# Two-layer attention and expert kernel on one core: split expert weights kept in DRAM, crossbar transposes in the ternary layer, expert groups of 64 rows in two lanes

## The chip, the cores and the metric

One Trainium2 chip, one core of it. The metric is the device time of one execution in microseconds (us), the median of several. Engines are called PE (matrix), PEld (its weight load), DVE (vector), ACT (scalar), POOL (GpSimd) and SP (the queue that issues most DMAs).

## The reference

Four blocks follow each other on x of 2 x 1024 tokens by 512, each as `x = layernorm(x + block(x))`:

```
x = _layernorm(x + _L0_attn_ref(...))   # causal attention, 32 query heads, 8 key heads, rope
x = _layernorm(x + _L0_ffn_ref(...))    # ternary layer, 512 -> 2048 -> 512
x = _layernorm(x + _L1_attn_ref(...))   # linear attention, 16 heads, silu gates
x = _layernorm(x + _L1_ffn_ref(...))    # 16 experts, 2 per token, plus a shared expert

def bitlinear(x, w):                    # the ternary layer's product
    xn = layer_norm(x)                  # then clipped a little under its row's largest |x|
    return einsum('bsd,od->bso', absmax_quant(xn), ternarize_weights(w))
h = gelu(bitlinear(x, w_fc)); y = bitlinear(h, w_proj)

gu = einsum('th,ehj->etj', x, w_gate_up)        # j = 2 x 352
y = einsum('eti,eih,te->th', silu(g) * u, w_down, combine) + swiglu(x @ shared_gate_up) @ shared_down
```

## The kernel before, in words

Tokens are worked on in 16 tiles of 128 rows. fp32 values enter matmuls as a high and a low fp16 part; a product of two split operands takes three matmuls (high-high, high-low, low-high). Each stage is a `Phase` with one hand-written instruction stream per engine. `run_tiles` and `unrolled` write a software pipeline: in iteration s the pair (lag, fn) works on tile s - lag, in the order in which the pairs stand in the list, so that this list is the order of the engine's queue. Semaphores tie the streams; `after` waits for a buffer to come free. The stages are: preparation, twice (projection, attention, output), `ternary_ffn` (lines 804 to 966), `linear_weights`, twice (`linear_features`, `linear_output`), `route`, `dispatch`, `sparse_experts` (1737 to 1944) and `shared_and_combine`.

In `ternary_ffn` a tile's row goes through x_stats and x_norm (with the clip at line 800) on DVE, the high part on ACT (893) and the low part on POOL (957), 8 transposes on PE and a copy out of PSUM on DVE (926), 32 matmuls (849), gelu on ACT (900), statistics and h_norm (717, 794, 800) on DVE, high part on ACT (906), low part on POOL (962), 32 transposes on PE (861), copied out of PSUM half by ACT (908) and half by DVE (885), 32 matmuls (871), residual and norm on DVE.

In the last block `route` picks two experts per token, and `dispatch` sorts the 4096 token-expert pairs into groups of GS = 128 rows that belong to one expert each, while PE computes the first half of the shared expert. There are NG = 48 groups, since an expert's last group may be part empty. `owner` holds each group's expert; `fresh` is 1 where it differs from that of the group before. `sparse_experts` takes a group per step, from STREAMS = 3 streams in turn: stream r works through groups 16r to 16r + 15 and has its own weight buffers. SP reads owner and fresh into registers and issues the loads of the fp32 weights, which are skipped where fresh is 0 (`cond`). In every step, loaded or not, ACT and DVE split the 128 x 2816 gate-up weights and the down weights into high and low parts (1857, 1863, 1864, 1905, 1921, 1923). PE order of a step: first half of the gate-up product, transposes of the hidden rows, second half, transposes of the next tokens, down product:

```
unrolled(NG, [(2, gate), (3, tr), (2, up), (1, xt), (3, down)])             # PE
unrolled(NG, [(1, gate_lo), (2, swiglu), (1, xevac), (2, down_lo)])         # DVE
unrolled(NG, [(1, gate_hi), (2, tanh), (3, hevac), (2, down_hi), (2, hhi), (3, yevac)])  # ACT
```

`shared_and_combine` computes the second half of the shared expert, whose weights are loaded and split at the end of `sparse_experts`, and gathers the expert rows.

## Time and profile before

| | |
|---|---|
| median of 3 runs | 2094.9 us (2094.39 to 2102.55) |
| the profiled execution | 2098.51 us, its span 2096.7 us, mean granted clock 0.93 |
| PE, DVE, ACT, POOL busy | 80%, 70%, 48%, 27% of the span |
| DMA | 105.96 MB, mean 51 GB/s |
| ternary_ffn, first to last instruction | 774.8 to 1103.8 |
| linear_features, twice | 1129.1 to 1223.0, 1281.7 to 1374.4 |
| dispatch | 1491.2 to 1591.0 |
| sparse_experts | 1594.3 to 1975.9 |
| shared_and_combine | 1987.2 to 2091.4 |

The span runs from the first to the last instruction of the profiled execution; the metric of that execution is 1.8 us longer. The parts after the table's stages are barriers and the smaller stages. A group of instructions is named by its line in the kernel, its engine, and the tensors written and read.

### The profile page before, as it was taken

Reading aid. Unit: us, or ns where it says so; the run is one execution under the profiler, and the core shown is the slowest. Engines: PE = TensorE matmul, PEld = TensorE weight load, DVE = VectorE, ACT = ScalarE, POOL = GpSimd, SP = SyncE. Lnnn points to the kernel's source line nnn. Section 1 sums busy time; section 2 is a strip of 40 time slices with the busy share of each in tenths; the row PEclk is TensorE's granted clock in tenths of the full one; section 3 lists DMA queues with packets and bytes.
Section 4 is the critical chain, followed back from the end, with each engine's and each line's share of the span. In section 5 each row is a group of like instructions: output and inputs, shape, how many; then the busy total and the mean of one; then the engine's idle time right before and its main releaser. Section 6 shows DMA issues by size and latency. Waiting matters only on the chain. (4 is left out here: it accounts for less than half of the span.)

```text
span 2096.7 us, 35409 instructions
## 1 busy us (share of the span) xinstructions
PE 1678.1 (80%) x13401; PEld 864.9 (41%) x13401; DVE 1463.9 (70%) x2115; ACT 997.4 (48%) x1549; POOL 571.1 (27%) x568
## 2 busy tenths in 40 slices
PE   0579999777999858888984977974696888888697
PEld 0353333344333223444441543543463555555364
DVE  3558998446898478999963364364624999999667
ACT  4345777434677713333333222222133777777532
POOL 0250000252000033344321122123261444444255
PEclk9889999998999989999996988996798999999899
DMA  8000000000000000000002000002004665345234
GB/s 298 1 2 2 2 2 2 1 1 1 2 2 2 2 1 1 1 0 0 1 1 91 1 1 1 1 1 96 32 2 144 195 195 153 113 154 183 94 102 139
DMA packets 49393, 105.96 MB, mean 51 GB/s; under 512 B 7096, under 2 KB 10392, under 8 KB 48720
## 3 DMA queue, kind: packets, MB, share of 16 engines
q1 hardware_dynamic: 37632, 75.99, 10.4%
q0 software_dynamic: 7424, 21.00, 3.9%
q10 hardware_dynamic: 4176, 6.82, 0.9%
q8 instruction: 103, 1.69, 0.3%
q14 instruction: 58, 0.48, 0.1%
HBM read 149.68 MB, written 21.01 MB: 81 GB/s over the span
## 5 line engine op out<-in xcount | busy, mean ns | idle before, releaser
L624 ACT ACTIVATE attn_prob<-attn_ps_t 128x512 f32<-128x512 f32 x576 | 312.6, 595 | 127.9 <-PE attn_ps_t L591 126.3
L643 DVE TENSOR_REDUCE attn_mx<-attn_ps_s 128x2 f32<-128x1024 f32 (+3 forms) x304 | 342.8, 1163 | 41.5 <-PE attn_ps_s L572 38.0
L136 PE MATMUL sparse_ps_g<-sparse_wg,sparse_xT 128*128 128x352 f16 x1152 | 190.5, 316 | 54.7 <-DVE sparse_xT L1900 54.7
L604 PE MATMUL attn_ps_o<-attn_prob,V 128*32 128x256 f32 x2304 | 174.8, 389 | 3.6 <-ACT attn_prob L624 2.7
L1905 DVE SCALAR_TENSOR_TENSOR sparse_wg<-sparse_raw_g,sparse_wg 128x2816 f16<-128x2816 f32 x48 | 148.4, 3092 | 37.9 <-ACT sparse_wg L1857 37.8
L136 PEld LDWEIGHTS sparse_ps_g<-sparse_wg,sparse_xT 128*128 128x128 f16 x1152 | 107.8, 99 | 128.8 <-DVE sparse_xT L1900 77.7
L778 POOL TENSOR_TENSOR wo_o<-O,wo_o 128x512 f16<-128x512 f32 (+1 forms) x16 | 18.4, 1153 | 496.0 <-ACT wo_o L750 495.9
L1942 POOL TENSOR_TENSOR sparse_h<-sparse_hid,sparse_h 128x352 f16<-128x352 f32 x48 | 87.7, 1826 | 217.4 <-ACT sparse_h L1876 217.4
L1021 PE MATMUL lin_ps_z<-w,lin_xT 128*128 128x512 f16 x576 | 136.2, 387 | 0.0
L1857 ACT ACTIVATE sparse_wg<-sparse_raw_g 128x2816 f16<-128x2816 f32 x48 | 122.0, 2541 | 17.2 <-DMA sparse_raw_g<-in_L_ffn_w_gate_up_dram 17.2
L849 PE MATMUL ffn_ps_fc<-wfcT,ffn_xT 128*128 128x512 f16 x512 | 123.6, 393 | 8.1 <-DVE ffn_xT L926 8.1
L591 PE MATMUL attn_ps_t<-QT,KT 64*128 64x256 f16 x1152 | 112.3, 273 | 18.6 <-ACT attn_prob L624 11.4
L871 PE MATMUL ffn_ps_y<-wprojT,ffn_hT 128*128 128x512 f16 x512 | 116.2, 386 | 10.6 <-issue 8.8
L572 PE MATMUL attn_ps_s<-KT,QT 64*128 64x512 f16 (+3 forms) x768 | 115.2, 336 | 2.1 <-DVE attn_mx L643 2.1
L1845 PE MATMUL sparse_ps_y<-sparse_wd,sparse_hT 128*128 128x512 f16 (+1 forms) x432 | 102.7, 383 | 1.0 <-ACT sparse_hT L1883 1.0
L908 ACT ACTIVATE ffn_hT<-ffn_ps_h 128x1024 f16<-128x1024 f16 x32 | 32.8, 1024 | 138.2 <-PE ffn_ps_h L861 138.2
L1021 PEld LDWEIGHTS lin_ps_z<-w,lin_xT 128*128 128x128 f16 x576 | 53.3, 99 | 70.3 <-issue 15.6
L591 PEld LDWEIGHTS attn_ps_t<-QT,KT 64*128 64x128 f16 x1152 | 39.0, 94 | 100.0 <-ACT attn_prob L624 45.1
L871 PEld LDWEIGHTS ffn_ps_y<-wprojT,ffn_hT 128*128 128x128 f16 x512 | 50.0, 99 | 71.4 <-issue 14.2
L604 PEld LDWEIGHTS attn_ps_o<-attn_prob,V 128*32 128x32 f32 x2304 | 49.3, 108 | 69.9 <-issue 37.5
L849 PEld LDWEIGHTS ffn_ps_fc<-wfcT,ffn_xT 128*128 128x128 f16 x512 | 49.9, 100 | 65.7 <-DVE ffn_xT L926 8.9
L962 POOL TENSOR_TENSOR ffn_h<-ffn_hn,ffn_h 128x2048 f16<-128x2048 f32 x16 | 65.0, 4065 | 37.4 <-ACT ffn_h L906 37.4
(320 smaller groups left out, 3407.2 us busy)
## 6 DMA issues: line engine op xcount, KB each, us to landing
sparse_raw_g<-in_L_ffn_w_gate_up_dram SPq DMA_DIRECT2D x48, 1408.0 KB
sparse_raw_d<-in_L_ffn_w_down_dram SPq DMA_DIRECT2D x48, 512.0 KB
y_d<-sparse_y SPq DMA_DIRECT2D x48, 256.0 KB, 3.6
sparse_raw_d<-in_L_ffn_w_down_dram SPq DMA_DIRECT2D x48, 192.0 KB
prep_w_fc<-in_L_ffn_w_fc_dram SPq DMA_DIRECT2D x4, 1024.0 KB, 15.6
X<-in_L_attn_x_dram ACTq DMA_DIRECT2D x1, 4096.0 KB, 39.6
prep_w_proj<-in_L_ffn_w_proj_dram SPq DMA_DIRECT2D x4, 1024.0 KB, 22.4
x_d<-route_x SPq DMA_DIRECT2D x16, 256.0 KB, 2.0
```

The source lines that it names most:

```text
L136: last = pe.matmul(out, a(k), b(k), start=(k == 0 and n == 0), stop=(k == chunks - 1 and n == 2))
L572: last = pe.matmul(banks[par][:, h, :], QT[s, pair + h, qt * P:(qt + 1) * P], KT[s, (pair + h) // 2, c * 512:c * 512 + n], start=not diago ...
L591: last = pe.matmul(ps_t[:, (2 * g + par) % 3, i, :], KT[s, j, kt * P:(kt + 1) * P], QT[s, 2 * j:2 * j + 2, qt * P:(qt + 1) * P], start=kt ...
L604: last = pe.matmul(ps_o[32 * jj:32 * jj + 32, 256 * half:256 * half + 256], V[:, kt, 4 * jg + jj, :], prob[(2 * q + jj // 2) % 4][:, half, ...
L624: act.activation(prob[g % 4][:, par, :, :], ps_t[:, (2 * g + par) % 3, :, :], ACT.Exp, scale=HD ** -0.5).then_inc(exp_done, 1)
L643: dve.tensor_reduce(mx[x % 2][:, c, :, at:at + per], ps_s[:, 2 * (r % 2):2 * (r % 2) + 2, 0:per * n].rearrange("p e (h k) -> p e h k", k=n ...
L849: last = pe.matmul(ps_fc[n][:, :], xT[u][:, part, k, :], m.wfcT[:, k, n * D:(n + 1) * D], start=(k == 0 and part == 0), stop=(k == KC - 1 ...
L871: last = pe.matmul(ps_y[:, :], hT[u][:, part, k, :], m.wprojT[:, k, :], start=(k == 0 and part == 0), stop=(k == NK - 1 and part == 1))
L1021: last = pe.matmul(out, xT[:, a, k, :], m.w1[:, b, i, k, :], start=False, stop=(k == KC - 1 and n == 2))
L1845: last = pe.matmul(ps_y[u][:, :], hT[u][0:size, a, k, :], wd[u][0:size, c, k, :], start=(k == 0 and n == 0), stop=(k == 2 and n == 2))
L1857: act.activation(wg[u][:, 0, :, :], raw_g[r][:, :, :], ACT.Copy, scale=WS).then_inc(gh_done, 1)
L1905: dve.scalar_tensor_tensor(wg[u][:, 1, :, :], raw_g[r][:, :, :], WS, wg[u][:, 0, :, :], ALU.mult, ALU.subtract).then_inc(gl_done, 1)
```

## The change

Three edits.

**The ternary layer** is written out without loops. Both transposes leave PE: SP issues one crossbar DMA transpose of a tile's x parts (128 x 1024 fp16) and two of its hidden parts (128 x 2048 fp16 each), from SBUF to SBUF. The copies out of PSUM go. The 128 x 2048 normalisation moves from DVE to ACT (scale and bias per row, the bias made by a small product on POOL), both low parts move from POOL to DVE, the second product has two PSUM banks, and the lags are shorter (down product at 6 instead of 7).

**The expert weights** are split once. `ExpertSplit` takes 7 pieces per expert (four of gate-up, three of down) through a ring of 6 buffers: SP loads a piece, ACT makes the high part, DVE the low part, SP stores both to DRAM tables `gate_d` and `down_d`. Experts 0 to 5 are done during the first `linear_features` (42 pieces over 8 tiles), 6 to 11 during the second, 12 to 15 and the shared second half during `dispatch` (35 pieces over 10 of its iterations). There, the work stands last in each iteration of ACT and DVE.

**The sparse stage** has groups of 64 rows, 80 of them, in STEPS = 40 steps: lane 0 takes the first 40 groups on rows 0 to 63, lane 1 the last 40 on rows 64 to 127, each with three streams. Weights come split, so ACT and DVE convert nothing. Each product is a pair of matmuls with a 64-column stationary operand, one per lane, which write the two halves of the PSUM partitions. SP reads owner and fresh for every lane and for gate-up and down apart. The low part of the hidden rows moves from POOL to DVE. The shared expert's second half is loaded after the last output.

```
-GS = P
+LANES = 2
+GS = P // LANES
 STREAMS = 3
-NG = -(-(B * N * TOPK // GS + NE - 1) // STREAMS) * STREAMS
+STEPS = -(-(B * N * TOPK // GS + NE - 1) // LANES)
+NG = LANES * STEPS
 MOST = B * N // GS
...
-    return s % STREAMS * (NG // STREAMS) + s // STREAMS
+    return sum(len(range(r, STEPS, STREAMS)) for r in range(s % STREAMS)) + s // STREAMS
...
+            @block.sync
+            def _(sp):
+                def xt(t):
+                    u = t % 2
+                    sp.wait_ge(xh_done, t + 1)
+                    sp.wait_ge(xl_done, t + 1)
+                    after(sp, fc_done, (t - 1) * NB)
+                    sp.dma_start_transpose(out=xT[u][:, :, :, :].rearrange("p a k c -> p (a k) c"),
+                                           in_=x2[u][:, :, :].rearrange("p a n -> p (a n)")).then_inc(xt_in[u], 16)
+
+                def ht(part):
+                    def fn(t):
+                        u = t % 2
+                        sp.wait_ge(hl_done if part else hh_done, t + 1)
+                        after(sp, y_done, t - 1)
+                        sp.dma_start_transpose(out=hT[u][:, part, :, :], in_=h2[u][:, part, :]).then_inc(ht_in[u][part], 16)
+                    return fn
+
+                unrolled(NT, [(3, xt), (5, ht(0)), (5, ht(1))])
+
...
+                def proj(t):
+                    u = t % 2
+                    after(pe, r_done, t - 1)
                     for part in range(2):
+                        pe.wait_ge(ht_in[u][part], 16 * (t // 2 + 1))
                         for k in range(NK):
-                            last = pe.matmul(ps_y[:, :], hT[u][:, part, k, :], m.wprojT[:, k, :],
+                            last = pe.matmul(ps_y[u][:, :], hT[u][:, part, k, :], m.wprojT[:, k, :],
                                              start=(k == 0 and part == 0), stop=(k == NK - 1 and part == 1))
...
+                unrolled(NT, [(4, fc), (6, proj)])
...
+                def h_norm(t):
+                    u = t % 2
+                    act.wait_ge(shift_done, t + 1)
+                    after(act, hl_done, t - 1)
+                    act.activation(hn[u][:, :], h[u][:, :, :].rearrange("p n k -> p (n k)"), ACT.Identity,
+                                   scale=ln_h.rstd[u][:, :], bias=shift[u][:, :]).then_inc(hn_done, 1)
+
+                unrolled(NT, [(4, gelu(0, 1, 2, 3)), (5, hhi), (2, xhi), (4, h_norm)])
...
+                    dve.tensor_tensor(x2[u][:, 1, :], xn[u][:, :], x2[u][:, 0, :], ALU.subtract).then_inc(xl_done, 1)
...
+                def h_clip(t):
+                    dve.wait_ge(hn_done, t + 1)
+                    q_h.apply(dve, hn[t % 2][:, :], t, t % 2)
+
+                def hlo(t):
+                    u = t % 2
+                    dve.wait_ge(hh_done, t + 1)
+                    after(dve, ht_in[u][1], 16 * (t // 2))
+                    dve.tensor_tensor(h2[u][:, 1, :], hn[u][:, :], h2[u][:, 0, :], ALU.subtract).then_inc(hl_done, 1)
...
-                turn = lambda g: evacuate(dve, dve.tensor_copy, ht_evac_d, g)
-                run_tiles(dve, NT, [(6, h_norm), (9, norm), (8, residual), (7, turn(1)), (5, h_stats), (7, turn(3)),
-                                    (3, x_evac), (1, x_norm), (0, x_stats)])
...
+                unrolled(NT, [(5, h_clip), (8, norm), (7, residual), (1, x_norm), (4, h_stats), (5, hlo), (2, xlo), (0, x_stats)])
...
-                run_tiles(pool, NT, [(8, lambda t, u: ln_r.root(pool, t, u)), (5, lambda t, u: ln_h.root(pool, t, u)),
-                                     (6, hlo), (2, xlo), (0, lambda t, u: ln_x.root(pool, t, u))])
+                def h_root(t):
+                    u = t % 2
+                    after(pool, hn_done, t - 1)
+                    pool.wait_ge(ln_h.s_var, t + 1)
+                    pool.tensor_tensor(ln_h.rstd[u][:, :], ln_h.var[u][:, :], m.minus_half[:, :], ALU.pow).then_inc(ln_h.s_rstd, 1)
+                    pool.wait_ge(back_done, t + 1)
+                    pool.wait_ge(ln_h.s_rstd, t + 1)
+                    pool.tensor_tensor(shift[u][:, :], back[u][:, :], ln_h.rstd[u][:, :], ALU.mult).then_inc(shift_done, 1)
+
+                unrolled(NT, [(7, lambda t: ln_r.root(pool, t, t % 2)), (4, h_root), (0, lambda t: ln_x.root(pool, t, t % 2))])
+
...
+class ExpertSplit:
...
+    RING = 6
...
+    def load(self, sp, i):
+        e, k, kd, rows, width = self.piece(i)
+        after(sp, self.lo_done, i - self.RING + 1)
...
+    def store(self, sp, i):
+        e, k, kd, _, width = self.piece(i)
+        sp.wait_ge(self.lo_done, i + 1)
...
+        sp.dma_start(table[e * P:(e + 1) * P, at * 2 * width:(at + 1) * 2 * width],
+                     self.parts[i % self.RING][:, 0:2 * width]).then_inc(self.stored[i % self.RING], 16)
+
+    def transfers(self, sp):
+
+        lag = self.RING - 2
+        for i in range(self.count + lag):
+            if i < self.count:
+                self.load(sp, i)
+            if i >= lag:
+                self.store(sp, i - lag)
...
+    def high(self, act, i):
+        u, turn = i % self.RING, i // self.RING
+        _, _, _, rows, width = self.piece(i)
+        act.wait_ge(self.raw_in[u], 16 * (turn + 1))
+        after(act, self.stored[u], 16 * turn)
+        act.activation(self.part(i, 0), self.raw[u][0:rows, 0:width], ACT.Copy, scale=WS).then_inc(self.hi_done, 1)
+
+    def low(self, dve, i):
+        _, _, _, rows, width = self.piece(i)
+        dve.wait_ge(self.hi_done, i + 1)
+        dve.scalar_tensor_tensor(self.part(i, 1), self.raw[i % self.RING][0:rows, 0:width], WS, self.part(i, 0),
+                                 ALU.mult, ALU.subtract).then_inc(self.lo_done, 1)
+
...
+    def spread(self, fn, eng, tiles, slot=0, slots=1):
+
+
+        def at(t):
+            turn = t * slots + slot
+            for i in range(turn * self.count // (tiles * slots), (turn + 1) * self.count // (tiles * slots)):
+                if t < tiles:
+                    fn(eng, i)
+        return at
 
...
+        split = ExpertSplit(f, m, d, b * LIN_EXPERTS, LIN_EXPERTS)
...
-                run_tiles(act, TB, [(0, xhi), (2, nonlinear), (3, kt_hi)])
+                unrolled(TB, [(0, of(xhi)), (2, of(nonlinear)), (3, of(kt_hi)), (0, split.spread(split.high, act, TB))])
...
-                run_tiles(dve, TB, [(1, xevac), (2, features), (3, kt_lo)])
+                unrolled(TB, [(1, of(xevac)), (2, of(features)), (3, of(kt_lo)), (0, split.spread(split.low, dve, TB))])
...
+                pe.wait_ge(m.shared_in, 32)
...
+        split = ExpertSplit(f, m, d, 2 * LIN_EXPERTS, NE + 1 - 2 * LIN_EXPERTS)
...
+                unrolled(NT, [(1, lambda t: half.swiglu(dve, t)), (4, split.spread(split.low, dve, 10, 0, 2)), (1, table_part),
+                              (3, lambda t: half.accumulate(dve, t)), (4, split.spread(split.low, dve, 10, 1, 2))])
...
+                split.transfers(sp)
...
+                def weights(s, rows, bufs, sem):
+                    r = s % STREAMS
+                    for lane in range(LANES):
+                        g = lane * STEPS + group_of(s)
                         e = sp.value_load(m.owner[0:1, g:g + 1], min_val=0, max_val=NE - 1)
                         fresh = None
                         if s >= STREAMS:
                             fresh = sp.value_load(m.fresh[0:1, g:g + 1], min_val=0, max_val=1)
+                        sp.dma_start(bufs[lane][r][:, :], rows[bass.ds(e, 1), :, :].rearrange("e p n -> p (e n)"),
+                                     cond=fresh).then_inc(sem[r], 16)
+
+                def gates(s):
+                    after(sp, gu_done, 2 * (s - STREAMS) + 2)
+                    weights(s, gate_rows, m.wgate, g_in)
+
+                def downs(s):
+                    after(sp, y_done, s - STREAMS + 1)
+                    weights(s, down_rows, m.wdown, d_in)
+
+                def outputs(s):
+                    sp.wait_ge(y_evac, s + 1)
+                    sp.dma_start(y_rows[group_of(s)], y[s % 2][:, :]).then_inc(y_out[s % 2], 16)
+
+                unrolled(STEPS, [(0, gates), (1, downs), (5, outputs)])
+                free = (STEPS - STREAMS) % STREAMS
+                sp.wait_ge(y_done, STEPS - STREAMS + 1)
+                sp.dma_start(m.wgate[0][free][:, :], gate_rows[NE]).then_inc(m.shared_in, 16)
+                sp.dma_start(m.wdown[0][free][:, :], down_rows[NE]).then_inc(m.shared_in, 16)
...
+                    for k in range(KC):
+                        for i, (a, c) in enumerate(((0, 0), (0, 1), (1, 0))):
+                            for lane, rows in enumerate(lanes):
+                                w = m.gate_part(m.wgate[lane][r], c, k, n)
+                                last = pe.matmul(ps_g[u][n][rows, :], xT[u][:, a, k, rows], w,
+                                                 start=(k == 0 and i == 0), stop=(k == KC - 1 and i == 2),
+                                                 skip_group_check=LANES > 1)
+                    last.then_inc(gu_done, 1)
...
-                    pe.wait_ge(gl_done, t + 1)
+                    pe.wait_ge(g_in[t % STREAMS], 16 * LANES * (t // STREAMS + 1))
...
-                unrolled(NG, [(2, gate), (3, tr), (2, up), (1, xt), (3, down)])
+                unrolled(STEPS, [(2, gate), (3, tr), (2, up), (1, xt), (3, down)])
...
-                unrolled(NG, [(1, gate_hi), (2, tanh), (3, hevac), (2, down_hi), (2, hhi), (3, yevac)])
-                shared_high(act, m, shared_g, raw_d[free], w_in, wh_done)
+                unrolled(STEPS, [(2, tanh), (3, hevac), (2, hhi), (3, yevac)])
...
+                unrolled(STEPS, [(2, swiglu), (2, hlo), (1, xevac)])
```

How the instructions stand on three engines, before and now. On DVE, the end of an iteration of the ternary layer, before (L885 and L926 are copies out of PSUM, ffn_hn the normalised hidden rows):

```order
L885 COPY ffn_hT<-ffn_ps_h 128x1024
L700 BN_STATS ffn_lnh_stats<-ffn_h 128x6 x4
L703 MEMSET ffn_lnh_pad 128x1
L704 BN_AGGR ffn_lnh_mv<-ffn_lnh_stats 128x2
L706 TENSOR_SCALAR ffn_lnh_var<-ffn_lnh_mv 128x1
L885 COPY ffn_hT<-ffn_ps_h 128x1024
L926 COPY ffn_xT<-ffn_ps_x 128x1024
L717 TENSOR_SCALAR ffn_xn<-X,ffn_lnx_mv,ffn_lnx_rstd 128x512
```

and now:

```order
L702 BN_STATS ffn_lnh_stats<-ffn_h 128x6 x4
L705 MEMSET ffn_lnh_pad 128x1
L706 BN_AGGR ffn_lnh_mv<-ffn_lnh_stats 128x2
L708 TENSOR_SCALAR ffn_lnh_var<-ffn_lnh_mv 128x1
L937 TENSOR_SCALAR ffn_back<-ffn_lnh_mv 128x1
L947 TENSOR_TENSOR ffn_h<-ffn_hn,ffn_h 128x2048
L930 TENSOR_TENSOR ffn_x<-ffn_xn,ffn_x 128x512
```

The copies are gone and the two low parts (L947, L930) have come from POOL; L717 of the hidden rows has left DVE.

On PE, a step of the sparse stage, before:

```order
L136 MATMUL sparse_ps_g<-sparse_wg,sparse_xT 128x352 x12
L1810 MATMUL sparse_ps_x<-ident,sparse_xg 128x128 x8
L1845 MATMUL sparse_ps_y<-sparse_wd,sparse_hT 128x512 x9
L136 MATMUL sparse_ps_g<-sparse_wg,sparse_xT 128x352 x12
L1835 MATMUL sparse_ps_h<-ident,sparse_h 128x128 x2
```

and now:

```order
L1930 MATMUL sparse_ps_g<-wgate,sparse_xT 64x352 x24
L1920 MATMUL sparse_ps_x<-ident,sparse_xg 128x128 x8
L1962 MATMUL sparse_ps_y<-wdown,sparse_hT 64x512 x18
L1930 MATMUL sparse_ps_g<-wgate,sparse_xT 64x352 x24
L1950 MATMUL sparse_ps_h<-ident,sparse_h 128x128 x2
```

The order is the same; the products have twice the matmuls on half the rows, and the transposes between them stay whole.

On SP, from one output to the next gate-up load, before:

```order
L1798 DMA y_d<-sparse_y 128x512
L1778 TENSOR_LOAD owner
L1778 ISA x2
L1781 TENSOR_LOAD fresh
L1781 ISA x2
L1783 ISA
L1783 DMA sparse_raw_g<-in_L_ffn_w_gate_up_dram 128x4x704
```

and now:

```order
L1902 DMA y_d<-sparse_y 2x64x512
L1885 TENSOR_LOAD owner
L1885 ISA x2
L1888 TENSOR_LOAD fresh
L1888 ISA x2
L1889 ISA
L1889 DMA wgate<-gate_d 128x5632
L1885 TENSOR_LOAD owner
L1885 ISA x2
L1888 TENSOR_LOAD fresh
```

The sequence from owner to DMA, once per step before, now stands four times between two outputs (two lanes, gate-up and down).

## Rows read from the trace of the kernel before

**Rows 1.** Stages: stretch, length, busy PE, PEld, DVE, ACT, POOL, clock, DMA, GB/s:

```profile
774.00:1105.00 331.00, 272.99 (x1664) 139.33 (x1664) 291.68 (x480) 112.24 (x129) 122.58 (x80) 0.95 0.00 1
1129.00:1226.00 97.00, 90.49 (x472) 45.03 (x472) 34.18 (x54) 25.72 (x45) 17.50 (x16) 0.94 0.00 1
1490.00:1594.00 104.00, 96.67 (x627) 57.65 (x627) 42.35 (x85) 28.75 (x64) 44.94 (x48) 0.98 0.02 2
1594.00:1983.00 389.00, 318.68 (x2256) 186.34 (x2256) 341.15 (x290) 292.00 (x387) 146.30 (x96) 0.97 0.52 166
```

**Rows 2.** Groups of DVE in the sparse stage (busy us, mean ns, idle before):

```profile
L1905 DVE SCALAR_TENSOR_TENSOR sparse_wg<-sparse_raw_g,sparse_wg 128x2816 f16<-128x2816 f32 x48 | 148.4, 3092 | 37.9 <-ACT sparse_wg L1857 37.8
L1921 DVE SCALAR_TENSOR_TENSOR sparse_wd<-sparse_raw_d,sparse_wd 128x1024 f16<-128x1024 f32 x48 | 58.4, 1216 | 0.0
L1900 DVE COPY sparse_xT<-sparse_ps_x 128x1024 f16<-128x1024 f16 x48 | 32.9, 686 | 0.0
```

**Rows 3.** Timeline of PE: start us, us, work, [idle before]; sparse stage, then the next:

```profile
1608.11 4.29 PE L136 MATMUL sparse_ps_g<-sparse_wg,sparse_xT 128*128 128x352 f16 x14 [6.72 <-DVE sparse_xT L1900]
...
1814.30 1.95 PE L136 MATMUL sparse_ps_g<-sparse_wg,sparse_xT 128*128 128x352 f16 x12
1816.53 2.11 PE L1845 MATMUL sparse_ps_y<-sparse_wd,sparse_hT 128*128 128x512 f16 x9
1819.67 1.96 PE L136 MATMUL sparse_ps_g<-sparse_wg,sparse_xT 128*128 128x352 f16 x12 [1.03 <-DVE sparse_xT L1900]
1821.86 1.36 PE L136 MATMUL sparse_ps_g<-sparse_wg,sparse_xT 128*128 128x352 f16 x8
...
1987.18 5.14 PE L136 MATMUL moe_ps_g<-ws_g,xT 128*128 128x352 f16 x17 [11.88 <-PEq L106]
```

**Rows 4.** Timeline of PE: fp32 matmuls on quarters and on all columns:

```profile
250.37 0.64 PE L604 MATMUL attn_ps_o<-attn_prob,V 128*32 128x256 f32 x8
250.94 0.39 PE L572 MATMUL attn_ps_s<-KT,QT 64*128 64x512 f16 x2
...
1154.86 1.05 PE L1065 MATMUL lin_ps_kv<-lin_v,lin_k 128*128 128x128 f32 x8
1155.74 0.60 PE L1072 MATMUL lin_ps_k<-consts,lin_k 128*128 128x128 f32 x4
```

**Rows 5.** Groups of PE's weight loads, by form:

```profile
L1835 PEld LDWEIGHTS sparse_ps_h<-ident,sparse_h 128*96 128x96 f16 x96 | 11.8, 123 | 0.0
L604 PEld LDWEIGHTS attn_ps_o<-attn_prob,V 128*32 128x32 f32 x2304 | 49.3, 108 | 69.9 <-issue 37.5 <-ACT attn_prob L624 25.9
```

**Rows 6.** Timeline of SP's DMA issues in the sparse stage, and its register loads:

```profile
1618.82 0.07 SPq L1789 DMA_DIRECT2D sparse_raw_d<-in_L_ffn_w_down_dram  x1
1620.34 0.07 SPq L1783 DMA_DIRECT2D sparse_raw_g<-in_L_ffn_w_gate_up_dram  x1
...
1739.51 0.34 SPq L1798 DMA_DIRECT2D y_d<-sparse_y  x1
1742.01 0.07 SPq L1783 DMA_DIRECT2D sparse_raw_g<-in_L_ffn_w_gate_up_dram  x1
...
L1781 SPq TENSOR_LOAD <-fresh x45: 261/1012/1132, 1603.6 to 1945.1; - x45
```

**Rows 7.** Ternary layer: groups, then min/median/max ns of single instructions:

```profile
L800 DVE TENSOR_SCALAR ffn_xn<-ffn_xn,ffn_qx_limit 128x512 f32<-128x512 f32 x16 | 43.3, 2706 | 0.6
...
L717 DVE TENSOR_SCALAR ffn_hn<-ffn_h,ffn_lnh_mv,ffn_lnh_rstd 128x2048 f32<-128x2048 f32 x16 | 28.6, 1787 | 0.8 <-issue 0.6
...
L800 DVE TENSOR_SCALAR ffn_xn<-ffn_xn,ffn_qx_limit x16: 545/4331/4428, 778.1 to 1006.6; 128x512 f32<-128x512 f32 x16
...
L962 POOL TENSOR_TENSOR ffn_h<-ffn_hn,ffn_h x16: 4057/4066/4073, 814.5 to 1084.2; 128x2048 f16<-128x2048 f32 x16
```

**Rows 8.** DMA: a stretch at full load, then a queue's packets, MB, share in 160:380:

```profile
20.00:40.00 20.00, 0.00 (x0) 0.00 (x0) 5.56 (x2) 18.46 (x17) 0.00 (x0) 1.00 1.03 404
...
q1 hardware_dynamic: 1062, 0.06, 0.3%
```

325 lines of the change are left out of this document (140 added, 185 removed).

## Prediction

> **What bounds the kernel now.** I read the stages first [rows 1], then inside the two stages that change most the groups of instructions and the timelines.
>
> In the sparse stage DVE is busy 341 of 389 us and PE 319. One step takes 7.56 us: the second gate-up halves start at 1814.30 and 1821.86 [rows 3]. Of it DVE spends 3.09 + 1.22 us on two of the three low parts of weights and 0.69 on a copy [rows 2]; the third low part and the gating fill the rest. PE waits 1.03 us per step for DVE's copy [rows 3], so alone it would need 6.5 us. DVE, chained to ACT's conversions, bounds the stage; 48 steps pay the conversion, although the experts are 16.
>
> In the ternary layer DVE is busy 292 of 331 us and PE 273. Part of DVE's time is not its own: the clip of 128x512 takes 0.545 us at best and 4.33 in the median, about the 4.07 of POOL's low part, beside which it runs [rows 7]. In linear features PE is busy 90 of 97 us, DVE 34 and ACT 26, in dispatch PE 97 of 104 [rows 1]: PE bounds both, and nothing moves over the DMA.
>
> **Ternary layer.** From DVE's 291.7 us go: the stalls of the clip, 16 x (2.706 - 0.545) = 34.6; the normalisation, 28.6 [rows 7]; 48 copies (32 of hidden, 16 of x) of the form that takes 0.686 [rows 2], 32.9. It gets both low parts. 128x1024 takes 1.216 and 128x2816 3.092 [rows 2], that is 1.05 ns per element, so 128x2048 costs 2.29 and 128x512 about 0.69; with 0.15 for the bias's sign, 16 x 3.13 = 50. Sum 245.6, **46 less**. PE loses 40 transposes per tile and keeps 64 matmuls of 128x512, about 64 x 0.215 = 13.8 us (9 such matmuls take 2.11 with the 0.17 of the last one's drain [rows 3]), under DVE's 15.3. ACT gets 1.9 us per tile and loses two copies. POOL keeps only one-column work. The order of the lists hides ACT's normalisation behind DVE's low parts (4.0 us), but leaves nothing over; I take 46, and 30 to 56 as its ends.
>
> The transposes have no row. Lower bound: 1.25 MB per tile at the 404 GB/s of a loaded DMA [rows 8], 3.2 us. Upper bound: the smallest packets of the trace, 64 bytes, 1062 of them in 0.3% of 16 engines over 220 us [rows 8], or 10 ns each: if a transpose goes in such packets, 20480 of them over 16 engines are 12.8 us. Both lie under 15.3 us per tile, and the lags leave about 7 us of slack behind a transpose, so it costs nothing. If it goes in 32-byte pieces, it is 25.6 us and bounds the layer (rival C). I take the hidden case, since the source is read along rows of 2 and 4 KB.
>
> The Trainium skill speaks against this change: VectorE: DVE Perf Modes, "The three transpose paths", gives 1309 ns for a 128x128 block by DMA against 390 on PE. Taken as a rate, 40 blocks are 52 us per tile and the sum would be 590 us worse. DMA: Bandwidth & Descriptors, "Latency and other measured facts", gives 261 GB/s, which would be 5 us per tile and hidden. No row here shows either; I read the first as a latency.
>
> **Splitting.** An expert has four 128x704 and three 128x512 pieces: DVE 4 x 0.88 + 3 x 0.68 = 5.6 us by the same line [rows 2]. Six experts in 97 us of linear features bring DVE from 34 to 68 us, ACT likewise from 26 to about 57, both under PE's 90. DMA: 6 x (2.11 read + 2.23 written) = 26 MB, 65 us at 404 GB/s. Covered in the middle; if that cover fails, the stage goes to the DMA's pace. At the start it isn't: five pieces (1.8 MB, 4.5 us, and 2 of latency) must land and be split before ACT makes the next tile's high part, on which PE's second transposes wait. Twice 6 us, and 2 each for late chunks: **+16** (+8 to +60). Dispatch gets 28 us of DVE over ten iterations of 6 us, and 22 MB, 54 us of DMA in them: **+5** (0 to +25).
>
> **Sparse stage.** POOL's low part goes to DVE, whose step is then about 2.2 us; ACT's is 2.5. Three candidates remain.
> PE: 24 pairs of gate-up, 9 of down, 14 transposes. If the lanes of a pair run beside each other, the step is PE's 6.5 us. Do they? Eight fp32 matmuls of 256 columns on quarters of the array start at 250.37 and are over at 250.94, 0.57 us; eight of 128 columns on the whole array take 0.88 [rows 4], so 256 columns one after another would take 1.76. Four quarters give 3.1 of 4. Bounds per step therefore 6.5 and, at that 0.77, 8.2; switching between halves and whole array four times a step, I take 7.1.
> SP: from the end of the y issue at 1739.85 to the end of the next gate-up issue at 1742.08 it takes 2.23 us, of which the fresh load is 1.01; without a DMA just ahead the same sequence takes 1.50 (1618.89 to 1620.41) [rows 6]. With nothing else on SP, it now stands four times a step: 2.23 + 3 x 1.50 + 0.38 for y = 7.1. An issued load adds 0.3, and 0.75 to the fresh load after it. 16 experts over six lane streams are at most 21 loads of each kind, 15 after the first six: 30 x 0.9 over 37 steps, 0.7. **SP needs 7.8 us per step** and is, narrowly, the bound.
> DMA: 21 x 2.2 MB, y and the gathers, some 68 MB in 310 us, under 404 GB/s; a buffer has two steps to fill.
> With the two interfering, 7.9 us. The stage: 12 us to the first gate-up (loads of 2.9 MB; 13.8 now, 1594.3 to 1608.1 [rows 3]), 8 for a first step at half clock, 36 x 7.9 = 284, 12.5 for the last step's tail, 3 for filling three buffers: 320 against 382, **-62** (-95 to -40).
> Then the shared weights: PE starts 11.9 us after its last sparse matmul [rows 3]; now there is no conversion, but the load (6 us and latency) starts after the last output: **-3**.
>
> **Sum.** -46 + 16 + 5 - 62 - 3 = -90, from 2098.5 of the profiled execution 2008.5; it stood 3.6 above the median, so 2005. A measurement tells 0.5%, 10 us, from no change.
>
> **Rivals.**
> A, neither SP nor lanes cost what I say: PE's 6.5 to 7.1 is the pace, 36 x 1.0 less: 1970. For it: fresh loads of 0.26 occur [rows 6]; against: their median is 1.01. Chance 0.17.
> B, the weight loads of the lanes don't hide. A load of 96 columns takes 123 ns, one of 32 columns 108 [rows 5]. If two of 123 go in turn before each pair, a step is 33 x 0.246 + 0.8 = 8.9, or 9.3 with the switches: 36 x 1.4 = +50: 2055. Against: in 0.57 us eight loads of 108 ns were done [rows 4, 5], so they overlap. The Trainium skill, TensorEngine Tiling (Array Packing), "Restrictions", says that column tiling switches fast weight load off. Rows 5 agree as far as they go (96 columns, 123 ns); by this rule it would be the 2055 of this rival. Chance 0.08.
> C, slower than before: the transposes at 25.6 us per tile pace the ternary layer, 16 x (25.6 - 15.3) = +165: 2170. It decides from 15.3 us per tile, and eats the whole gain from 21 (by the VectorE page's figure, above, it would be 2595). Chance 0.08.
> D, also slower: the lanes of a pair run in turn. 24 x 0.149 + 9 x 0.213 = 5.5 us more than 6.5, 12.0 per step: 36 x 4.1 = +148: 2153. Rows 4 speak against it. Chance 0.04.
> E, splitting stalls: the bursts on ACT and DVE, in order ahead of each tile's work, wait for pieces still in the DMA, 20 us in each of two stages: 2045. For it: five pieces per burst and a ring of six. Chance 0.10.
>
> **Numbers.** Forecast 0.53, 1980 to 2035. The range takes in A, B and E and leaves out C, D and part of A: 1960 to 2065. Faster: forecast, A, B, E, together 0.88, less 0.02 for several together: 0.86; same 0.03; slower 0.11 (C, D).
>
> **What would show it.** Ternary layer 283 us, DVE at 0.9 busy and the clip at 0.55 us; if PE waits for the DMA transposes there, C. Linear features 102 us each, PE's first z later by 6. Sparse stage 320 us, steps of 7.9 whose gate-up waits on SP's loads that were skipped; a pair of 128x352 matmuls at 0.15 to 0.19 us. If PE has no wait there, A or B by the pair's time. I am wrong if SP's sequences are shorter in a row of four, or if splitting costs more than its start.

## The result, and the profile after

The changed kernel takes 2123.1 us (median of 4 runs, 2120.4 to 2125.3) against 2094.6 of the kernel before in the same comparison: ratio 1.0127, 95% interval 1.0099 to 1.0155, 1.3% slower. The forecast was 2005 with a range of 1960 to 2065. The profiled execution of the changed kernel has a span of 2120.3 us.

The stages of the changed kernel, in the columns of [rows 1] (ternary layer, the two linear features, dispatch, sparse stage):

```profile
773.20:1056.10 282.90, 234.55 (x1024) 101.13 (x1024) 232.26 (x463) 111.22 (x113) 63.98 (x64) 0.93 0.42 75
1081.60:1181.00 99.40, 89.84 (x472) 44.89 (x472) 62.92 (x91) 50.26 (x82) 19.01 (x16) 0.92 0.75 266
1239.90:1338.80 98.90, 89.09 (x472) 44.69 (x472) 63.03 (x91) 48.82 (x81) 19.28 (x16) 0.93 0.76 267
1457.50:1596.20 138.70, 107.72 (x627) 60.00 (x627) 70.09 (x122) 50.40 (x99) 49.30 (x48) 0.89 0.71 160
1600.40:1997.20 396.80, 305.08 (x3200) 185.29 (x3200) 86.80 (x160) 89.11 (x200) 37.68 (x40) 0.89 0.47 171
```

From the first to the last instruction of each stage, in both traces:

| stage | before | after | difference | forecast |
|---|---|---|---|---|
| ternary layer | 329.0 | 282.9 | -46 | -46 |
| linear features, both | 186.6 | 198.3 | +12 | +16 |
| dispatch | 99.8 | 138.7 | +39 | +5 |
| sparse stage | 381.6 | 396.8 | +15 | -62 |
| gap to the shared expert's first product | 11.3 | 14.8 | +3.5 | -3 |

The span grew by 23.6 us, and the rows add up to 23.5. Two terms carry nearly the whole error: dispatch, and above all the sparse stage. There DVE, which bounded the stage before [rows 1], is busy 87 of 397 us, and PE 305; nobody is busy enough to be the bound. The waits of that stage (engine, line, waited for, us in total, times, longest):

```profile
DVE sparse_hid L2010 <- ACT sparse_th L1975: 261.6, 40, 10.4
ACT sparse_y L1994 <- DMA y_d<-sparse_y: 252.1, 38, 10.6
PE sparse_ps_y L1962 <- ACT sparse_hT L1988: 71.9, 32, 6.2
```

ACT's evacuation of a result waits for the store of y two steps earlier, 252 us; ACT works in order, so the tanh of the next step stands behind it, and DVE and PE behind that. The page's chain that ended last begins the same way:

```profile
DMA y_d<-sparse_y 9%; PE moe_ps_g L138 3%; SPq L1885 2%; SPq L1888 2%; PE moe_ps_y L1567 1%; PE sparse_ps_y L1962 1%; PE sparse_ps_g L1930 1%; SPq L1889 1%; DMA wgate<-gate_d 1%; DMA wdown<-down_d 1%; ACT sparse_y L1994 0%; PE moe_ps_h L1558 0%; SPq L1902 0%; DMA moe_yg<-y_d,slot 0%; ACT sparse_hT L1987 0%
```

One step in the timeline (start, us, work, idle before): a store is issued at 1795.72, and the evacuation two steps on, which waits for it, comes at 1808.66 after 8.58 us of waiting; the hidden transposes' copy follows at 1809.49, and PE's down product at 1810.42. The store issued at 1806.80 is the next one, for which the evacuation at 1819.62 waits. The 18 matmuls of the down product take 3.58 us, where the same 18 take 2.13 in the runs below without the idle time ahead: the granted clock is 0.58 from 1810.4 to 1814.0, so they went mostly at the lower of the clock's two levels. Over the stage it is 0.89.

```profile
1795.72 0.56 SPq L1902 DMA_DIRECT2D y_d<-sparse_y  x1
...
1806.80 0.56 SPq L1902 DMA_DIRECT2D y_d<-sparse_y  x1
1808.66 0.60 ACT L1994 ACTIVATE sparse_y<-sparse_ps_y 128x512 f32<-128x512 f32 x1 [8.58 <-DMA y_d<-sparse_y]
1809.49 0.60 ACT L1987 ACTIVATE sparse_hT<-sparse_ps_h 128x512 f16<-128x512 f16 x1
1810.42 3.58 PE L1962 MATMUL sparse_ps_y<-wdown,sparse_hT 128*64 128x512 f16 x18 [2.66 <-ACT sparse_hT L1988]
...
1818.19 0.56 SPq L1902 DMA_DIRECT2D y_d<-sparse_y  x1
1819.62 0.60 ACT L1994 ACTIVATE sparse_y<-sparse_ps_y 128x512 f32<-128x512 f32 x1 [8.37 <-DMA y_d<-sparse_y]
```

From issue to landing a store takes 12.5 us here: by the trace's packets the first moves at 1803.09 and the last is over at 1808.24. In the middle stores of the stage the median is 8.2 us, against 3.7 in the kernel before. The wait names the store, but not what about it is late: its place in SP's list (issued five iterations later, four before), the rate of SP's list, or the transfer itself. The experiments tell these apart.

In dispatch, over 1490 to 1575, the queue that carries the pieces is full, at a rate far below the 404 GB/s of [rows 8]; the median landing of a piece's store is 11.5 us against 4.0 in the linear features:

```profile
DMA packets 9767, 18.61 MB, mean 219 GB/s; under 512 B 1837, under 2 KB 2861, under 8 KB 9762
q1 hardware_dynamic: 8866, 18.53, 100.8%
gate_d<-disp_sp_parts SPq DMA_DIRECT2D x17, 352.0 KB, 11.5
```

### The profile page after: what moved, and what is told of

Same layout as the page of the kernel before. It is cut to its first block and busy times, and to the rows that moved or that the text cites. A ratio compares the mean times of both kernels' runs of the same rounds, so it can differ in the third digit from the quotient of the medians.

```text
span 2120.3 us, 36564 instructions
## 1 busy us (share of the span) xinstructions
PE 1634.4 (77%) x13705; PEld 828.0 (39%) x13705; DVE 1238.1 (58%) x2090; ACT 867.1 (41%) x1465; POOL 411.2 (19%) x496
## 5 line engine op out<-in xcount | busy, mean ns | idle before, releaser
L2010 DVE SCALAR_TENSOR_TENSOR sparse_hid<-sparse_th,sparse_ps_g 128x352 f32<-128x352 f32 x40 | 20.9, 521 | 261.6 <-ACT sparse_th L1975 261.6
L1930 PE MATMUL sparse_ps_g<-wgate,sparse_xT 128*64 128x352 f16 x1920 | 164.7, 323 | 9.6 <-issue 5.1
L1962 PE MATMUL sparse_ps_y<-wdown,sparse_hT 128*64 128x512 f16 (+1 forms) x720 | 108.6, 459 | 71.9 <-ACT sparse_hT L1988 71.9
L1930 PEld LDWEIGHTS sparse_ps_g<-wgate,sparse_xT 128*64 128x64 f16 x1920 | 108.4, 114 | 58.4 <-issue 13.0
L868 PE MATMUL ffn_ps_fc<-wfcT,ffn_xT 128*128 128x512 f16 x512 | 115.2, 384 | 17.4 <-DMA ffn_xT<-ffn_x 16.4
L1994 ACT ACTIVATE sparse_y<-sparse_ps_y 128x512 f32<-128x512 f32 x40 | 23.9, 597 | 255.1 <-DMA y_d<-sparse_y 252.1
L2030 POOL DMA_INDIRECT sparse_xg<-x_d,token x40 | 37.7, 942 | 332.9 <-PE sparse_ps_x L1920 321.5
L1962 PEld LDWEIGHTS sparse_ps_y<-wdown,sparse_hT 128*64 128x64 f16 (+1 forms) x720 | 44.0, 128 | 120.1 <-ACT sparse_hT L1988 77.6
L1119 PEld LDWEIGHTS lin_ps_z<-w,lin_xT 128*128 128x128 f16 x576 | 53.1, 99 | 69.9 <-issue 14.8
L909 ACT ACTIVATE ffn_hn<-ffn_h,ffn_shift,ffn_lnh_rstd 128x2048 f32<-128x2048 f32 x16 | 33.5, 2093 | 109.7 <-POOL ffn_shift L971 109.7
L1053 DVE SCALAR_TENSOR_TENSOR lin_sp_parts<-lin_sp_raw,lin_sp_parts 128x704 f16<-128x704 f32 (+2 forms) x84 | 63.6, 804 | 22.8 <-ACT lin_sp_parts L1048 22.8
```

What stands on the lines that cost most here:

```text
L868: last = pe.matmul(ps_fc[n][:, :], xT[u][:, part, k, :], m.wfcT[:, k, n * D:(n + 1) * D], start=(k == 0 and part == 0), stop=(k == KC - 1 ...
L1053: dve.scalar_tensor_tensor(self.part(i, 1), self.raw[i % self.RING][0:rows, 0:width], WS, self.part(i, 0), ALU.mult, ALU.subtract).then_in ...
L1119: last = pe.matmul(out, xT[:, a, k, :], m.w1[:, b, i, k, :], start=False, stop=(k == KC - 1 and n == 2))
L1930: last = pe.matmul(ps_g[u][n][rows, :], xT[u][:, a, k, rows], w, start=(k == 0 and i == 0), stop=(k == KC - 1 and i == 2), skip_group_chec ...
L1962: last = pe.matmul(ps_y[u][rows, :], hT[u][0:size, a, k, rows], w, start=(k == 0 and i == 0), stop=(k == 2 and i == 2), skip_group_check=L ...
```

## The experiments

### The place of the store: one step earlier, or four buffers

```
-                unrolled(STEPS, [(0, gates), (1, downs), (5, outputs)])
+                unrolled(STEPS, [(0, gates), (1, downs), (4, outputs)])
```

> Edit: in the sparse stage SP issues the store of y for step s one step of its list earlier (lag 4 in place of 5); nothing else moves. Theory (the store of y stands too late in SP's queue, and with two buffers y the evacuation on ACT waits for it): after's sparse stage takes 396.8 us, 9.9 us a step, and y_d<-sparse_y ends ACT's idle time for 252 us. One step of lead less takes most of that wait away; the step falls to SP's own list, 7.0 to 8.5 us, the stage to 290 to 340 us, and the kernel to 2035 to 2065 us. Rival (SP's register loads and its conditional issues bound the step by themselves, the wait for y is only where it shows): the wait moves to the weights' DMAs and the stage stays within 10 us of 397, the kernel at 2110 to 2125.

Measured: 2084.1 us, ratio to the kernel before 0.995 (0.9932 to 0.9968); the stage 358.6 us. Less than the theory gave, and ACT still waits 175 us for the store.

```
-        y = [f.sb(f"y{u}", [P, D], F32) for u in range(2)]
+        y = [f.sb(f"y{u}", [P, D], F32) for u in range(4)]
...
-                    after(act, y_out[u], 16 * (t // 2))
+                    after(act, y_out[t % 4], 16 * (t // 4))
```

> Edit: y has four buffers and four semaphores in place of two, the store stays where it was (lag 5). Theory of the late store: ACT's evacuation no longer waits for it, the loop through SP's queue is cut, stage 290 to 340 us, kernel 2035 to 2065 us, about as the run with lag 4. Rival (SP's rate): stage within 10 us of 397. A second rival (SP's queue blocks through its waits on up and down, so that weights come late whatever the store does): ACT no longer waits for y, PE waits for g_in or d_in in its place, stage 350 to 385 us.

Measured: 2075.5 us, 0.9897 (0.9875 to 0.9919); the stage 343.0 us, just outside what the theory gave, and the kernel 10 us outside. ACT's wait for the store is down to 24 us, and long stretches now run at PE's pace. In its place PE waits for weights, which is what the second rival said, with a longer stage:

```profile
PEld sparse_ps_g L1930 <- issue: 48.9, 14, 6.1
ACT sparse_y L1994 <- DMA y_d<-sparse_y: 23.6, 9, 4.3
```

At the end of the stage the gap to the shared expert is 25 us instead of 14.8, which no theory had. SP's issues there: five issues of stores take 16.4 us of SP, where one takes 0.55 elsewhere. The first two take 0.6 and 0.5 us, the last three 5.2, 5.0 and 5.0, and the load behind them 5.0 more.

```profile
1933.32 16.42 SPq L1902 DMA_DIRECT2D y_d<-sparse_y  x5
...
1949.78 4.97 SPq L1907 DMA_DIRECT2D wgate<-gate_d  x1
1954.80 0.52 SPq L1908 DMA_DIRECT2D wdown<-down_d  x1
1968.44 0.77 PE L138 MATMUL moe_ps_g<-wgate,xT 128*128 128x352 f16 x2 [27.80 <-DMA wdown<-down_d]
```

### The rate of SP's list

Both on the version with four buffers. First, the registers of a step are read once and kept for the down weights:

```
+                        if (s, lane) not in loaded:
+                            e = sp.value_load(m.owner[0:1, g:g + 1], min_val=0, max_val=NE - 1)
...
+                            loaded[s, lane] = e, fresh
+                        e, fresh = loaded[s, lane]
```

> Edit on the version with four buffers of y: SP reads owner and fresh of a step once, for its gate part, and keeps both registers for the down part one iteration later, so a step issues 4 register loads and their checks in place of 8. In the version with four buffers the undisturbed step is 6.76 us on PE, 40 of them are 270 us, and the stage took 343: PE waited 14 times, 1.2 to 5.6 us, for fresh gate weights that SP had issued only a step before their use, though the buffer had been free two steps longer. Theory (SP's list of about 7.9 us a step is longer than PE's 6.76, so SP runs late and the next real load is not ahead): four register loads and their checks less are 4 x (0.27 + 0.16 + 0.05) = 1.9 us, SP's step falls to about 6, the stage to 295 to 320 us, the kernel to 2030 to 2055 us. Rival (the loads of 1.4 MB land late because of the DMA's rate, 7 us each and two lanes together): stage within 8 us of 343.

Measured: 2060.1 us, 0.9832 (0.9815 to 0.9848); the stage 326.6, 16 less, short of the 295 to 320 expected. SP now waits 51 us for PE's products, so its list is no longer the bound, yet PE still stands up to 6.1 us ahead of fresh gate weights. The kernel too stays 5 us above its range.

Second, the store is issued by ACT:

```
-                unrolled(STEPS, [(0, gates), (1, downs), (5, outputs)])
+                unrolled(STEPS, [(0, gates), (1, downs)])
...
+                def outputs(t):
+                    act.wait_ge(y_evac, t + 1)
+                    act.dma_start(y_rows[group_of(t)], y[t % 4][:, :]).then_inc(y_out[t % 4], 16)
```

> Edit on the version with four buffers of y: the store of y is issued by ACT right behind its evacuation, not by SP. Theory of SP's rate: 0.56 us of issue and the wait behind it leave SP's list (of 0.92 us mean, the longest 5.2), SP's step falls by 0.6 to 1.0 us, the stage from 343 to 315 to 335 us; less than the register loads bring. ACT has 0.6 us more a step and idles more than half of it. Rival (DMA rate): within 8 us of 343.

Measured: 2069.8 us, 0.9879 (0.9863 to 0.9896); the stage 343.1, no gain: the rival's number, but neither the theory nor the rival had the reason. The issue of a store holds ACT, once for 12.6 us:

```profile
1755.22 12.58 ACTq L1994 DMA_DIRECT2D y_d<-sparse_y  x1
...
1767.91 0.47 ACT L1971 ACTIVATE sparse_th<-sparse_ps_g 128x352 f32<-128x352 f32 x1 [12.71 <-issue]
```

### No weights moved

This too is on the version with four buffers.

```
-                    done(dve.tensor_tensor(m.fresh[:, 1:NG], least[:, 1:NG], least[:, 0:NG - 1], ALU.is_gt))
+                    done(dve.tensor_tensor(m.fresh[:, 1:NG], least[:, 1:NG], least[:, 1:NG], ALU.is_gt))
```

> Edit on the version with four buffers of y: the flag that a group has another expert than the one before is always 0, so SP reads the same registers and issues the same conditional transfers, and none after the first three steps moves weights (the output is not the reference's). Theory (PE's 6.76 us a step is the floor, SP's list is longer than that only through the real transfers and the long register loads): stage 40 x 6.76 plus start, 280 to 295 us. Rival (SP's list alone, 7.5 us or more a step without any real transfer, is the bound): 300 us or more, with PE waiting at most steps.

Measured (one run): 2117.2 us, the stage 383.6, **41 us longer** than with the weights' traffic. The theory fell. The rival holds, at far more than its 300: SP waits 29 of 310 us on semaphores, its step is 9.4 us, PE stands ahead of the gate-up product in 30 steps, and ACT waits 148 us for the store again. SP's issues:

```profile
1804.99 0.55 SPq L1902 DMA_DIRECT2D y_d<-sparse_y  x1
1809.71 1.61 SPq L1889 DMA_DIRECT2D wgate<-gate_d  x2
1812.76 1.58 SPq L1889 DMA_DIRECT2D wdown<-down_d  x2
1814.38 0.55 SPq L1902 DMA_DIRECT2D y_d<-sparse_y  x1
```

Behind each store 4.2 us pass before the next gate issue (1805.54 to 1809.71), where behind other issues it is 1.4. They lie in the two register loads after the store, 0.86 and 2.31 us in the mean, against 0.26 to 0.33 for the other six. The line of the second one (minimum, median, maximum in ns) in this run:

```profile
L1888 SPq TENSOR_LOAD <-fresh x148: 261/266/2417, 1616.3 to 1972.1; - x148
```

So 2.7 us of SP's step stand behind the store and are not its own instructions. With the weights' traffic the second load can take 2.4 us too, but does so in few steps (mean 0.61 in the version with four buffers), which fits this run being the slower one; what decides it stays open. What is special about the store shows at the end of the changed kernel's stage, from 1975 to 2013, in 40 slices (tenths of the 16 DMA engines busy, and GB/s):

```profile
DMA  1156941111111111111111111979989511111100
GB/s 67 52 73 213 375 188 47 52 50 52 52 50 52 52 52 52 50 52 52 50 52 52 50 52 52 206 299 467 419 369 425 226 52 61 59 47 67 52 26 0
```

While only stores of y run, a tenth of the DMA engines is busy and 52 GB/s move: an eighth of the 404 of [rows 8], as if 2 of 16 engines worked. The packets say the same: 128 a store, of 2048 bytes and 84 ns each, and they start two by two every 0.08 us, 64 x 0.08 = 5.1 us. Four issues in a row of the run with four buffers (three stores and the load behind them) block for 5.0 to 5.2 us each, the time of one store. When the first of them blocks, two to three earlier stores have not landed, and not the four that the next expectation counts. The store's target is written as two blocks of 64 rows, so its outermost dimension is 2. In the kernel before it was 128 rows in one block, and landed in 3.7 us (median from 1750 to 1800) between other traffic.

### The form of the store

```
-                    sp.dma_start(y_rows[group_of(s)], y[s % 2][:, :]).then_inc(y_out[s % 2], 16)
+                    for lane, rows in enumerate(lanes):
+                        sp.dma_start(y_rows[group_of(s)][lane], y[s % 2][rows, :]).then_inc(y_out[s % 2], 16)
...
-                    after(act, y_out[u], 16 * (t // 2))
+                    after(act, y_out[u], 16 * LANES * (t // 2))
```

> Edit on the changed kernel, and this alone: each step's y goes out as two stores, one of 64 rows for each lane, in place of one store whose target is two blocks of 64 rows; two buffers, lag 5 as before. What speaks for it: at the end of the changed kernel's sparse stage, where nothing else moves, the stores of y run one after the other at 52 GB/s with a DMA share of 0.1 of the 16 engines, 5.1 us for 256 KB, where 12 to 15 GB/s for each of 16 would be over 200; the issue of a store behind four others then blocks SP for 5.0 us; and with no weights moved at all the stage still took 384 us. Theory Y (the store of two blocks is carried by about 2 of the 16 engines, 5.1 us each, and everything behind it on these engines waits): the stores land in 2 to 3 us, SP's list has one issue of 0.5 us more but loses the register loads of 0.85 and 2.3 us behind a store, the stage falls from 397 to 300 to 345 us with nothing else changed, the gap ahead of the shared expert from 14.8 to under 12, and the kernel to 2020 to 2070 us. Rival P (only the place of the store in SP's list counts): SP's list is 0.5 us longer, the stage 397 or more, the kernel 2120 to 2140.

Measured: 2049.4 us, 0.9788 (0.9772 to 0.9803), 74 us less than the changed kernel, with one issue more per step. Two buffers, the place and all register loads are as they were. The sparse stage of this run, in the columns of [rows 1], and the second register load's line:

```profile
1599.40:1928.90 329.50, 280.77 (x3200) 177.01 (x3200) 86.78 (x160) 89.88 (x200) 37.94 (x40) 0.96 0.60 207
```

```profile
L1888 SPq TENSOR_LOAD <-fresh x148: 259/264/737, 1617.1 to 1913.9; - x148
```

```profile
1802.08 1.10 SPq L1903 DMA_DIRECT2D y_d<-sparse_y  x2
1804.85 1.60 SPq L1889 DMA_DIRECT2D wgate<-gate_d  x2
...
1807.89 1.58 SPq L1889 DMA_DIRECT2D wdown<-down_d  x2
1809.52 1.09 SPq L1903 DMA_DIRECT2D y_d<-sparse_y  x2
```

The stage falls from 396.8 to 329.5 us, the granted clock rises from 0.89 to 0.96, the register load's maximum falls from 2.4 to 0.74 us, the time from the store to the gate issue is 1.7 us (4.2 in the run without weights' traffic), and the gap ahead of the shared expert is 9.5. A store of 64 rows lands 2.9 us after its issue in the median; its packets alone take 0.75 us where nothing else moves. Theory Y holds and rival P falls.

The wait that led here is not gone with it:

```profile
ACT sparse_y L1995 <- DMA y_d<-sparse_y: 168.3, 35, 8.0
```

The store lands soon after its issue now, but its issue comes at SP's pace, 7.4 us for the step above and 7.8 in the mean of the stage. With two buffers this wait is SP's list seen from ACT. The Trainium skill, DMA: Bandwidth & Descriptors, "Why a DMA increments its semaphore by 16 and not by 1", says that a DMA runs on the largest number of engines up to 16 that divides the slowest dimension of both its sides: 2 for two blocks of 64 rows, 16 for 64 or 128 rows. The 52 GB/s, the packets that start two by two and the run with two stores agree.

### Dispatch: whose time is it?

Loads left out except for the first six pieces, the rest of the splitting kept:

```
+        if self.first == 2 * LIN_EXPERTS * PIECES:
+            if i < self.RING:
+                k = i % KC
+                sp.dma_start(self.raw[i][:, :], self.d["L1_ffn_w_gate_up"][e, k * P:(k + 1) * P, :]).then_inc(sem, 16)
+            return
...
```

> Edit: in dispatch only the first six pieces of weights are loaded; the other 29 are split and stored from the same buffers, so the loads of 29 pieces are left out (the experts 12 to 16 get wrong weights), while ACT and DVE do the same work and the stores stay. Theory (dispatch, 138.7 us where before had 99.8, is bound by its DMAs: the engines of the DMA are busy 100% of it at 219 GB/s, and ACT's and DVE's lists stop at each piece that has not landed): half of the bytes go, the stage falls to 105 to 115 us, the kernel by 24 to 34 us to 2086 to 2099. Rival (the work of the splitting and its order on ACT and DVE holds back the tiles, not the transfers): the stage stays at 130 us or more and the kernel above 2110.

Measured: 2097.0 us; dispatch 109.1 us, as the theory has it. The splitting's instructions in the lists of ACT and DVE cost under 10 us, stores and scatters beside them.

Scatters left out, all but one:

```
-                    for b in range(4 * t, min(4 * t + 4, NB)):
+                    for b in range(4 * t, min(4 * t + 4, 1)):
...
-                pool.wait_ge(scattered, 16 * NB)
+                pool.wait_ge(scattered, 16)
```

> Edit: of the 32 scatters of token numbers in dispatch 31 are left out (so nearly every row of the sparse stage gathers token 0, and the output is not the reference's); all splitting stays. Question: the DMA moved 201 GB/s while the scatters ran and 266 GB/s after the last of them, against 270 GB/s in the stage of the linear features. Theory A (the scatters of single words slow the pieces' packets): the stage's pieces land at 260 to 280 GB/s, 24.8 MB take about 95 us, the stage falls by 15 to 30 us, the kernel to 2090 to 2108. Theory B (the scatters do not matter): within 5 us of the changed kernel.

Measured: 2093.6 us; dispatch 105.4 us, 33 less, a little more than theory A gave, with all 35 pieces loaded and stored, at 313 GB/s; a piece's store lands in 4.8 us (1485 to 1550). POOL's own work goes too (15 us busy in place of 49), but DVE and ACT are as busy as in the changed kernel (70 and 49 us), so it is not their instructions that got faster:

```profile
DMA packets 9839, 20.34 MB, mean 313 GB/s; under 512 B 1162, under 2 KB 2186, under 8 KB 9834
q1 hardware_dynamic: 9802, 20.28, 88.0%
gate_d<-disp_sp_parts SPq DMA_DIRECT2D x19, 352.0 KB, 4.8
```

Stores put off to the end of dispatch:

```
         sp.wait_ge(self.lo_done, i + 1)
+        if self.first == 2 * LIN_EXPERTS * PIECES and not late:
+            return
...
```

> Edit on the changed kernel: in dispatch the pieces are loaded and split but not stored while the tiles run; 35 stores of what is in the buffers then follow at its end (experts 12 to 16 get wrong weights). The loads, 12.4 MB, stay beside the 32 scatters. With loads left out the stores' packets took 174 ns each, and without scatters all packets 93 ns. Theory S (the scatters of words slow stores, not loads): the loads run at 90 to 110 ns a packet, DMA share well under 0.7, tiles of dispatch end 105 us after its start. Theory L (they slow every packet of the queues): 150 ns or more a packet and a share near 0.9, as with loads left out. The 35 stores at the end take 25 to 35 us more, and say by their own packets what stores take alone.

Measured (one run): 2115.3 us, tiles of dispatch over after 122 us. The loads alone, beside the scatters (1490 to 1560):

```profile
DMA packets 5546, 9.03 MB, mean 129 GB/s; under 512 B 1450, under 2 KB 2474, under 8 KB 5541
q1 hardware_dynamic: 4645, 8.95, 81.9%
```

That is 0.819 x 16 x 70 us / 4645 = 197 ns for a packet. The same sum gives 174 with loads left out, 155 in the changed kernel and 93 without scatters. The mix of sizes is not behind it: packets of 2816 bytes take 130 ns without scatters, and 200, 222 and 260 in the changed kernel, with loads left out and with stores put off. Theory L holds: loads and stores are both slowed. The additional time over 16 engines is (155 - 93) x 8866 / 16 = 34 us in the changed kernel, 26 with loads left out and 30 with stores left out, beside 28 to 32 scatters: about 1 us (0.8 to 1.2) of all the queue's engines for each scatter of 128 single words. That is the 33 us which the stage lost without them.

Fewer pieces beside the scatters, on the version with four buffers:

```
-LIN_EXPERTS = 6
+LIN_EXPERTS = 7
```

> Edit on the version with four buffers of y: each stage of linear features splits 7 experts in place of 6, dispatch 3 in place of 5 (21 pieces in place of 35). Theory (in dispatch the pieces' DMA goes at 219 GB/s while the scatters run, and it bounds the stage): dispatch falls from 138 to 103 to 115 us, as without scatters or without loads; the features' stages have 49 pieces at about 2 us each of DMA and rise by 2 to 8 us each. Kernel 2050 to 2068 us. Rival (the features' stages were at their limit, 2.36 us a piece): they rise by 16 us each and the kernel stays at 2075.

Measured: 2052.8 us (2041.4 to 2061.5 over 4 runs), 0.9808 (0.9784 to 0.9833), 23 less than the version with four buffers. Dispatch 102.7 us, near the 99.8 of before; the linear features 101.9 and 101.7, 2 more each.

### The ternary layer alone

```
-                run_tiles(pe, NT, [(4, of(fc, 0)), (7, of(ht, 0, 1)), (4, of(fc, 1, 2)), (7, of(ht, 2, 3)),
-                                   (4, of(fc, 3)), (3, xt), (7, proj)])
+                unrolled(NT, [(4, fc), (6, proj)])
...
+                unrolled(NT, [(3, xt), (5, ht(0)), (5, ht(1))])
```

> Edit on the kernel before: only the ternary layer is exchanged for the changed one; the splitting, the dispatch and the sparse stage stay as before. If the parts add up: stage 329 to 283 us, kernel 46 us below before, 2045 to 2052 us. If the transposes' 1.25 MB a tile or the shifted clock cost something later, it is less.

Measured: 2047.9 us, 0.9777 (0.9760 to 0.9793), 47 below the kernel before; the stage 283.0 us. The part is worth what it shows in its stage.

### Together

```
-                sp.wait_ge(y_done, STEPS - STREAMS + 1)
-                sp.dma_start(m.wgate[0][free][:, :], gate_rows[NE]).then_inc(m.shared_in, 16)
-                sp.dma_start(m.wdown[0][free][:, :], down_rows[NE]).then_inc(m.shared_in, 16)
...
+                    if s == STEPS:
+                        sp.wait_ge(gu_done, 2 * (STEPS - STREAMS) + 2)
+                        sp.dma_start(m.wgate[0][free][:, :], gate_rows[NE]).then_inc(m.shared_in, 16)
+                    if s == STEPS + 2:
+                        sp.wait_ge(y_done, STEPS - STREAMS + 1)
+                        sp.dma_start(m.wdown[0][free][:, :], down_rows[NE]).then_inc(m.shared_in, 16)
```

> Edit: four buffers of y, registers read once, 7 experts in each stage of linear features and 3 in dispatch, and at the end of SP's list the shared expert's gate weights are loaded as soon as the buffer is free (after the gate and up products of step 37), ahead of the last stores of y; its down weights two iterations later. If the parts add up: 2053 of the version with 7 experts, minus 15 for the registers, minus 10 to 20 for the gap between the sparse stage and the first product of the shared expert (25 us there, 11.3 in the kernel before): 2018 to 2035 us, 3 to 3.5% below the kernel before. Rival (the gap is the last y stores and the gathers, not the shared weights): 2035 to 2045.

Measured: 2044.7 us, 0.9771 (0.9754 to 0.9787), the rival's number: the gap stayed at 24.0 us although the shared weights were asked for three steps earlier, and dispatch came out at 110.8, not 102.7, for which no run gives the reason. It is the last stores, each 5.1 us behind the other, for which the end of the stage waits.

Then the same with the two stores of 64 rows:

```
-                    sp.dma_start(y_rows[group_of(s)], y[s % 4][:, :]).then_inc(y_out[s % 4], 16)
+                    for lane, rows in enumerate(lanes):
+                        sp.dma_start(y_rows[group_of(s)][lane], y[s % 4][rows, :]).then_inc(y_out[s % 4], 16)
```

> Edit: the combination run before (four buffers of y, registers read once, 7 experts in each stage of linear features and 3 in dispatch, the shared weights loaded early) with the two stores of 64 rows. Theory Y: the steps run at PE's 6.76 us with few waits for fresh weights, the stage takes 285 to 310 us where the combination took 331, the gap of 24 us to the shared expert falls to 8 to 12, kernel 2045 - 20 to 45 - 12 to 16: 1985 to 2013 us, 4 to 5% below the kernel before. Rival P: within 5 us of 2045.

Measured (5 runs): **1986.5 us, 0.9487 (0.9473 to 0.9500)**, 5.1% below the kernel before and 6.4% below the changed one. Against the combination above, only the form of the store differs, and with four buffers ACT waited for it only 14 us in 5 steps: the sparse stage falls from 331.2 to 294.4 us and the gap from 24.0 to 5.2, so what it held up there was mostly what SP issued behind it. The packets of the combination's trace show how. A lane's gate weights are 128 packets of 11264 bytes; of one load 112 move from 1790.6 to 1794.6, and the other 16, the eighth that 2 of 16 engines would carry, only from 1798.0 to 1801.8. At 1861.1 PE starts after 6.1 us of idle time, 1.0 us behind the last of such a group of 16. In the run with the two stores a load's packets move together, and the longest idle time ahead of a gate-up product, 4.0 us, lies in the start of the stage. In the steady part PE is the pace, 6.76 us from down product to down product, with nothing idle in between:

```profile
1763.76 2.13 PE L1977 MATMUL sparse_ps_y<-wdown,sparse_hT 128*64 128x512 f16 x18
1765.73 1.96 PE L1945 MATMUL sparse_ps_g<-wgate,sparse_xT 128*64 128x352 f16 x24
1767.62 0.51 PE L1965 MATMUL sparse_ps_h<-ident,sparse_h 128*128 128x128 f16 x6
1768.06 1.98 PE L1945 MATMUL sparse_ps_g<-wgate,sparse_xT 128*64 128x352 f16 x24
1769.97 0.62 PE L1935 MATMUL sparse_ps_x<-ident,sparse_xg 128*128 128x128 f16 x8
1770.52 2.13 PE L1977 MATMUL sparse_ps_y<-wdown,sparse_hT 128*64 128x512 f16 x18
```

## Why the forecast was wrong

**Ternary layer, -46: right in size, by two misses that cancel.** The clip takes 0.55 us in place of 2.71, DVE's low part of 128x2048 2.28 (2.29 forecast). But DVE is busy 232 us and not the 246 of the sum, 0.82 of the layer and not 0.9: the sum took back the stalls of one clip alone, and others went with them. The clip of 128x2048 took 1.74 us and takes 1.35, most normalisations of 128x512 took 0.99 and take 0.55. And ACT's normalisation, forecast as hidden, is not: DVE waits 26 us for it. The transposes don't bound the layer: their packets take 41.3% of 16 engines, 7.3 us per tile, between the bounds of 3.2 and 12.8, and PE waits 33 us in all for those of the hidden part (and 16 once, for the first of x), while DVE is busy 14.5 of the 16.2 us of a steady step.

```profile
L796 DVE TENSOR_REDUCE ffn_qh_g<-ffn_hn 128x1 f32<-128x2048 f32 x16 | 36.6, 2286 | 26.4 <-ACT ffn_hn L909 26.4
L878 PE MATMUL ffn_ps_y<-wprojT,ffn_hT 128*128 128x512 f16 x512 | 123.6, 398 | 33.2 <-DMA ffn_hT<-ffn_h 33.0
L947 DVE TENSOR_TENSOR ffn_h<-ffn_hn,ffn_h 128x2048 f16<-128x2048 f32 x16 | 36.5, 2282 | 0.0
L802 DVE TENSOR_SCALAR ffn_xn<-ffn_xn,ffn_qx_limit 128x512 f32<-128x512 f32 x16 | 8.7, 546 | 0.6
```

Rival C is out. The 1309 ns for a block of the Trainium skill (VectorE: DVE Perf Modes, "The three transpose paths"), taken as a rate, would be 52 us per tile; the trace's 16.2 us a step rules that reading out.

**Splitting in the linear features, +16: measured +12, for the reason given.** The stages take 99.4 and 98.9 us where 102 were forecast. PE waits for its second transposes as the forecast said, 7.00 us in place of 0.88, and its first z comes 6.1 us later (first line the kernel before, second the changed one):

```profile
1132.89 1.01 PE L144 MATMUL lin_ps_x<-ident,lin_x 128*128 128x128 f16 x8 [0.88 <-DVE lin_xT L1111]
1091.58 1.04 PE L146 MATMUL lin_ps_x<-ident,lin_x 128*128 128x128 f16 x8 [7.00 <-POOL lin_x L1252]
```

The 2 us each for late chunks did not come.

**Dispatch, +5: mis-sized, +39.** The step that failed is "22 MB, 54 us of DMA in them", a price at the rate of a DMA with nothing but large packets. The row of scatters was there to be read in the kernel before (32 of them in this stage), where nothing else was moved beside them. 33 of the 39 us are theirs. Rival E named splitting that stalls, with 20 us in each of two stages, but by the bursts of a ring of six; with the scatters gone the bursts cost 6 us.

**Sparse stage, -62: measured +15.** The working of the step itself held. The lanes of a pair run beside each other: 24 matmuls in 1.98 us, less the 0.17 of the last one's drain, are 151 ns a pair, and PE's step is 6.76 us within the 6.5 to 8.2 given. SP's list takes 7.8 us a step in the mean with the store mended, as forecast (its 30 x 0.9 for issued loads should be 30 x 1.05 by its own prices, 0.1 us a step), and the stage 329.5, 320 forecast. What failed is the line "0.38 for y": the store was priced by its issue, as in the kernel before, and its transfer left out, although the diff changes the target's view from rows of a group to two blocks. It takes 5.1 us on 2 of 16 engines in place of 16; with two buffers it holds the evacuation, and what SP issues after it gets slower too: register loads, and the eighth of each transfer that those 2 engines carry. Of the 77 us between forecast and result 67 are this form, by the run that changes only it.

**Shared weights, -3: measured +3.5, and -1.8 with the stores mended.** What came last was again the stores.

With the scatters' 33 us in it, the forecast's sum would have been 2038; the changed kernel with the store in two parts measured 2049. Rivals A, B and D are about lanes and SP and are out: A because SP did cost what was said, B and D by the 151 ns. None of the rivals had the form of a transfer in it, and the chance of 0.86 for faster took the priced parts for all there were.

## What to carry to other kernels

Price a transfer by the shape of both its sides, not by its bytes: a view whose outermost dimension is 2 went at an eighth of the rate here, and it delayed the loads issued behind it even where hardly anything waited for the store itself. When a change re-addresses a buffer in DRAM, look at every DMA that uses the new view, also those that seem unchanged. Before transfers are put under work that hides them, see what else uses the DMA there: scatters that cost nothing alone took about a microsecond each from all the rest. And a wait that names a transfer can be the issuing queue's pace: here the same wait was mostly the store's own time at first (8.2 us from issue to landing, in steps of 9.6) and then, with the store mended, SP's list (2.9 in steps of 7.8); the time from issue to landing tells the two apart.

## What the runs showed of the hardware

- A store of 256 KB to two blocks of 64 rows moves 52 GB/s, 5.1 us, its packets two at a time; two stores of 64 rows took the stage from 396.8 to 329.5 us.
- With two or three of these on their way, the issue of another blocked its engine: 5.0 to 5.2 us on SP for each at the end of the stage, once 12.6 on ACT. It didn't always: on ACT most issues with two on their way took 0.5 to 3.4 us. Moving the store to another engine only moved the block.
- A load of weights behind such a store came in two parts: 112 of its 128 packets in 4.0 us, the other 16 done 7.2 us after those.
- The two register loads behind such a store took 0.86 and 2.31 us in the run without weights' traffic, against 0.26 to 0.33 otherwise; the maximum of the second fell from 2.4 to 0.74 with the store in two parts. What the load waits for was not tried.
- A scatter of 128 single words beside large transfers took about 1 us from all of them: 155 to 197 ns a packet against 93, and 200 to 260 against 130 for packets of 2816 bytes, while the scatters' own queue showed 1% of the DMA's time.
- Pairs of matmuls on halves of the PE columns ran beside each other: 151 ns for two of 128x352, where one on all columns takes 0.149 (12 in 1.96 us, less the last one's drain).
